# Four state sums and two groups of transposes trade places in TensorE's queue

## The reference

```python
# mixer, for each batch: 1024 tokens in a row, 128 inner channels, 16 states
xs = silu(causal_conv(norm(x) @ in_proj));  delta = softplus(dt @ dt_proj + b)
dA = exp(delta * A[n]);  h[n] = dA * h[n] + (delta * xs) * B[n]     # along the tokens
y  = sum over n of h[n] * C[n]  + xs * D
x  = x + project(layer_norm((y * silu(z)) @ out_proj + skip * norm(x)))
# experts: each token goes to the expert with the largest logit
pos  = (how many earlier tokens chose the same expert);  kept = pos < capacity
x    = x + kept * prob * expert(norm(x))
```

## Time and profile before

| | |
|---|---|
| median of 3 runs | 378.38 us (378.09 to 379.71) |
| the profiled execution | 379.07 us, span 377.3 us (1.77 us lie around the span) |
| busy share of the span | DVE 81%, PE 80%, POOL 74%, ACT 62% |
| mean granted TensorE clock | 0.888 of full speed |

### The profile page before, as it was taken

The page is one execution under the profiler, slowest core; times in us unless marked ns, Lnnn a source line. Parts: engine busy times, 40 slices in busy tenths (PEclk is TensorE's granted clock), DMA queues, the critical chain, the costliest instruction groups (busy, mean ns, idle before and its releaser), DMA issues.

```text
span 377.3 us, 4331 instructions
## 1 busy us (share of the span) xinstructions
PE 302.6 (80%) x1257; PEld 178.5 (47%) x1257; DVE 307.1 (81%) x352; ACT 232.6 (62%) x519; POOL 278.4 (74%) x198
## 2 busy tenths in 40 slices
PE   7842788847988898998899697579988689999950
PEld 3321333213634344464436254436476357888940
DVE  5799999999999999999999979899998215755620
ACT  4455989623888984688898419856655145646320
POOL 3345669888894899989599988699997604477772
PEclk9975699996998989889899879989999759999985
DMA  4879999987999798859959685999961090000000
GB/s 92 146 173 359 321 343 324 300 270 241 275 295 339 295 320 304 257 178 340 364 146 341 219 242 136 339 304 341 217 107 31 20 276 12 4 20 16 22 12 0
DMA packets 48625, 78.68 MB, mean 209 GB/s; under 512 B 16210, under 2 KB 31373, under 8 KB 48602
## 3 DMA queue, kind: packets, MB, share of 16 engines
q1 hardware_dynamic: 46362, 76.54, 66.1%
q0 software_dynamic: 2240, 1.86, 1.6%
HBM read 72.30 MB, written 7.54 MB: 212 GB/s over the span
## 4 chain that ended last, share of the span: by engine, by line
DVE 56%; PE 18%; issue 10%; POOL 7%; ACT 3%; DMA 3%; DVEq 1%; POOLq 1%; ACTq 0%; SPq 0%
DVE h L1342 34%; DVE Bp L1289 15%; PE Cp L1162 5%; PE Bp L1176 4%; POOL slots L576 2%; POOL prod L534 2%; PE Yp L993 2%; POOL out_dram L626 2%; PE Bp L1151 1%; DMA csb<-slots 1%; DMA xs_in<-in_x_dram 1%; PE Yp L1193 1%; DVE h L1457 1%; POOL h L605 1%; PE Yp L1220 1%
## 5 line engine op out<-in xcount | busy, mean ns | idle before, releaser
L534 POOL TENSOR_TENSOR prod<-h,csb 128x1024 f32<-128x1024 f32 (+1 forms) x64 | 143.6, 2251 | 19.4 <-DVE h L1342 9.5
L993 PE MATMUL Yp<-prod,ident 128*128 128x512 f32 (+1 forms) x256 | 127.3, 634 | 13.7 <-POOL prod L534 13.5
L1342 DVE TENSOR_TENSOR_SCAN h<-dA,Bp 128x1024 f32<-128x1024 f32 (+2 forms) x58 | 119.7, 2064 | 4.9 <-POOL prod L534 1.2
L993 PEld LDWEIGHTS Yp<-prod,ident 128*128 128x128 f32 x256 | 50.6, 209 | 75.1 <-issue 51.3
L706 ACT ACTIVATE dA<-delta,aneg 128x1024 f32<-128x1024 f32 (+1 forms) x58 | 62.9, 1092 | 19.0 <-DVE h L1342 14.7
L1289 DVE TENSOR_TENSOR Bp<-Cp,bsb 128x1024 f32<-128x1024 f32 (+1 forms) x58 | 67.7, 1168 | 2.3
L626 POOL DMA_INDIRECT out_dram<-dA,csb x30 | 30.5, 1017 | 27.8 <-DVE dA L1533 20.8
L576 POOL DMA_INDIRECT slots<-rows_,slot x30 | 30.1, 1005 | 9.8 <-issue 5.4
L1521 DVE TENSOR_TENSOR dA<-Bp,b2s 128x320 f32<-128x320 f32 (+1 forms) x8 | 3.8, 475 | 22.0 <-PE Bp L1176 22.0
L1162 PE MATMUL Cp<-prod,w1s 128*128 128x384 f32 (+1 forms) x64 | 21.6, 462 | 0.0
L1176 PEld LDWEIGHTS Bp<-w2s,prod 128*128 128x128 f32 x152 | 18.1, 192 | 1.8 <-issue 0.3
(11 more groups left out here) (289 smaller groups left out, 592.0 us busy)
## 6 DMA issues: line engine op xcount, KB each, us to landing
bsb<-bc_rows SPq DMA_DIRECT2D x48, 512.0 KB, 6.1
csb<-bc_rows SPq DMA_DIRECT2D x48, 512.0 KB, 5.9
bsb<-bc_rows SPq DMA_DIRECT2D x16, 384.0 KB, 5.5
csb<-bc_rows SPq DMA_DIRECT2D x16, 384.0 KB, 5.1
csb<-slots SPq DMA_DIRECT2D x6, 325.0 KB, 5.2
slots<-fill SPq DMA_DIRECT2D x1, 1300.0 KB, 10.1
slots<-fill SPq DMA_DIRECT2D x10, 130.0 KB, 6.3
bcs<-bc_rows SPq DMA_DIRECT2D x2, 512.0 KB, 13.5
```

The costliest lines, as they stand in the source:

```text
L534: po.tensor_tensor(prod[:, k % 4, c], h[:, k % 3, c], csb[:, k % CSLOTS, c], ALU.mult).then_inc(s_pP, 1)
L993: ins = te_.matmul(Yp[:, c], idn, prod[:, k % 4, c], start=False, stop=(n == 15), skip_group_check=True)
L1342: ins = ve.tensor_tensor_scan(h[:, k % 3, c], decays, drives, h[:, k % 3, c.start - 1:c.start] if i else 0.0, ALU.mult, ALU.add)
```

## The change

TensorE's program is written in another order at two steps; no other engine's queue changes, and no instruction is added or removed.

```diff
                     if v and n in (5, 6, 11):
                         for stage in place(v - 1, n):
                             back(v - 1, stage)
+                    if n == 0 and v:
+                        add_state(v - 1, 15)
                     if v + 1 < B:
                         front(v + 1, n)
                         if n == 1:
                             pe.wait_ge(f_top, 2 * v + 3)
                         if n == 4:
                             pe.wait_ge(f_xcr, v + 1)
-                    if n == 0 and v:
-                        add_state(v - 1, 15)
+                    if n == 15:
+                        add_state(v, 13)
                     if v and n and n not in (5, 6, 11):
                         for stage in place(v - 1, n):
                             back(v - 1, stage)
                     if n > 1:
-                        add_state(v, n - 2)
-                    if n == 15:
-                        add_state(v, 14)
+                        add_state(v, n - 2 if n < 15 else 14)
```

## The result

The changed kernel takes 383.52 us (median of 6 runs, 382.37 to 384.67); the kernel before, beside it on the same chip, took 378.66 us (6 runs, 377.10 to 379.87). The ratio is 1.0133, with an interval of 1.0100 to 1.0166: about 5.0 us slower. The forecast was 379.6 us, with a range of 378.0 to 381.1, so the time lies outside it. The profiled execution of the changed kernel took 384.13 us, with a span of 382.4 us against 377.3 and a mean granted clock of 0.889 against 0.888. As that mean hardly moved, the loss is not a kernel that ran at a lower clock throughout.

The account below looks back on a forecast made before the run. DVE's own work was taken to set more than half of the end, TensorE counting only where DVE waits for it. The terms 1.6 + 0.35 + 0 - 0.7 + 0 = +1.25 us gave 379.6 us, range 378.0 to 381.1.

Parts of the forecast that it names:

- Transposes behind state 15: Borders of units 0/1 and 1/2: late transposes delay ACT's copies and decays, so state 2's scan comes 1.6 and 0.35 us later.
- The signs named for it: Unit 1: state 2's first half decay starts near 101.2, DVE idles about 1.6 us before that scan; unit 2: 0.2 to 0.5.
- The 0.35: Border of units 1 and 2: scan 0.2 to 0.45 us later, taken as 0.35 to allow for the hand-over.
- The gate of unit 2: Border of units 2 and 3: state 13 ahead of the rank products shortens the gate's 1.78 us wait; 0.7 us earlier taken.
- the two cases of the working: State 13's add in unit 2: at half clock a gain of 0.2 to 0.7 us, at full clock 1.78 us.
- Ranks of units 1 and 3: State 13 ahead of the rank products: 0 in each; up to 1.2 us in unit 1, 0.7 in unit 3 otherwise.
- the slow rival: Next unit: TensorE falls behind, ACT's step 4 copies wait, state 7's decay comes late; 1.6 us more, 381.2 us; chance 17%.
- the two idle times that the prediction saw: TensorE's idle times of 1.91 and 3.56 us, followed by slow adds, taken as agreeing with half clock after idling.

Follow-up runs that it names:

- the copies in time: The whole change, but with the eight transposes split: the first four ahead of state 15, the other four behind it; 379.5 us, ratio 1.0028.
- the control of the opening ahead of the projection: The kernel before, with the next sum opened ahead of the projection at the borders of units 0/1 and 1/2; 379.79 us, ratio 1.0026.
- the control of the early decay: The kernel before, with the decay of state 7 ahead of ACT's step 4 in units 1 and 2; 379.98 us, ratio 1.0013.
- the early decay: The whole change, with ACT making the decay of state 7 of units 1 and 2 ahead of its copies of step 4; 380.85 us, ratio 1.0042.
- state 13 alone: The kernel before, with only state 13 moved ahead of the rank products and state 15 left in its old place; 378.83 us, ratio 0.9999.
- both edits: The whole change, with the decay of state 7 ahead of ACT's step 4 and the next sum opened ahead of the projection; 382.28 us, ratio 1.0085.

## Why the prediction was wrong

- **Transposes behind state 15, 1.6 and 0.35 us: right in size.** DVE waited 1.50 and 0.29 us ahead of the scans of state 2, released by the decay that was named, and the kernel in which of the waits for ACT only these were left lost 1.6 us. The signs named for it came as well: the first half of state 2's decay started at 101.19 (forecast 101.2). The 0.35 rests on the move of state 13, which lets TensorE start earlier: in the two kernels that move state 15 at that border without it, state 2 of unit 2 waited 1.80 and 1.09.
- **The gate of unit 2, -0.7: nearly the right mechanism, a poor basis.** In the profiled execution the step gained 1.8: the add of state 13 took 2.55, between the two cases of the working, the ranks cost 0.40, and the gate no longer waited. Alone, the move gained nothing: the gate's wait was traded for the ranks', as the working had it at the lower clock. The basis was poor because the 1.78 of the earlier trace rows is not a fixed number: in the five other kernels that leave state 13 in its place the same gate waited 0.21 to 1.44, three times about 0.5. There is a slip in the working too: 2 x 1.8 is 3.6, not 3.5, so its range at half clock is 0.1 to 0.6, and the 0.7 that was taken lies above it.
- **Ranks of units 1 and 3, 0 and 0: right in the end.** Unit 3's ranks waited 1.08, and the gate and the norm behind them gave back 0.5 and 0.4.
- **The step that failed: the sum has no term for TensorE's wait for the late copies.** "DVE has next to no idle time between there and the border of units 2 and 3, so this is not made up" holds for DVE's own queue, but the sum took from it that the lateness is paid once. It followed the late copies down ACT's queue to state 2 and stopped. It did not follow them to the other reader of the same copies, the projection, and put that path at nothing. TensorE waited for them (1.22) and was 6.4 us late at the convolution; ACT's later copies, with the decays of states 5 and 7 queued behind them, made DVE pay again: 5.4 us by the ledger of the profiled execution. With the copies in time the loss was 0.28% in place of 1.33%, and with the decay of state 7 alone taken out of their way 0.42%.
- **This was the slow rival, "TensorE falls behind in the next unit", with a chance of 17% and a price too small.** Its place and its test were right: it "decides once TensorE's transposes of step 4 end later than ACT's second half of state 5", and ACT did stand idle for them, 2.67 us, behind those halves. But it was priced 1.6 for one unit, from one more slow opening of 1.5 us; the lag of TensorE was 6.4, and it was paid in both units. The argument against it, "unit 2 has had that stretch and did not wait", was a false comfort: the earlier trace rows show 0.14 us of room left, and unit 1, without that stretch, had only 0.35 by the same count (118.03 - 116.53 - 1.15). What ACT's decay is late beyond this room and beyond DVE's own lateness, DVE waits for: in unit 1 of the change it came 5.45 us later and DVE was 3.0 late, which makes 2.1 us, against 2.26 measured.

How much of the 5.4 us belongs to TensorE's late start itself and how much to the lower clock behind it was not measured apart: of the lag of 6.4, the one makes 2.28 and the other 4.1, but what room swallowed of each the runs don't tell. The 4.1 is at the upper end of what was seen: by the times of projection and opening, the eight moved borders ran 1.7 to 4.2 us slower than at full clock.

## What to carry to other kernels

When a producer is moved back in an in-order queue, list every reader of its result on every engine, and follow each one's own queue to the next place where it feeds the critical engine; a delay that is paid at the first reader can be paid again through the second. An engine that looks as if it had time may be filling a gap for another: the add of state 15 was the work under which ACT's copies were hidden, and half of the transposes ahead of it is enough to keep that cover. And a wait of one profiled execution is a poor ground for a gain, if it hangs on the clock: look at it in a second kernel or execution, and ask which instruction waits in its place.

## What was not expected of the hardware

In the change, TensorE's granted clock was 1.00 up to 99.5 us, fell about 1 us into the first matmuls of 64 columns, and stayed at 0.50 from 101.5 to 108.5 us, in which TensorE was busy without a break, 7.00 of 7.00 us. Eight transposes and an idle time of 1.22 us came just ahead of these matmuls; the kernel before had the same matmuls without the idle time and ran at 1.00. With the transposes split, an idle time of 1.22 us that a full-width add follows left the clock at 1.00, and so did one of 1.62 us that the opening follows (the control of the opening ahead of the projection, first border). But an idle time is not needed for a fall: in the control of the early decay the clock fell in the second half of the projection (0.72 in the mean from 99.0 to 101.6) with TensorE busy throughout. Nor does an idle time always bring one: the same wait of 2.97 to 2.98 us ahead of the add of state 13 in unit 2 was followed by an add of 1.98, 2.55, 3.13 and 3.78 us in four kernels (the split transposes, the change, state 13 alone, both edits). So the two idle times that the prediction saw followed by slow adds, 1.91 and 3.56 us, make no rule. Where the fall comes varies, with one and the same queue of TensorE, from the projection's first half (the change) to the opening (the early decay), and this may be a part of why runs of one and the same kernel spread over some 3 us (377.10 to 379.87 before); that it is the cause was not shown. No run here tells the part of the transposes from that of the idle time or of the narrow matmuls.
